# Fused four-block image kernel: the pieces of a normalised unit each one place later, four unit slots, loads two ahead

## The reference, cut to what matters

```python
x = x + L0(_gn(x))        # windowed attention with a roll
x = x + relu((y - mean(y)) * rsqrt(var(y) + eps) * gamma + beta)   # y = grouped 3x3 conv of _gn(x); mean over ALL images
x = x + L2(_gn(x))        # 1x1 conv, 3x3 conv in four chained groups, 1x1 conv
x = x + L3(_gn(x))        # the same once more
```

## Time and profile before

| | |
|---|---|
| median of three runs | 2432.0 us |
| the profiled execution, device time | 2433.68 us |
| its span in the trace | 2431.9 us |
| TensorE busy | 2062.5 us (85%) |
| VectorE busy | 1672.6 us (69%) |
| ScalarE busy | 1166.5 us (48%) |
| GpSimd busy | 1068.4 us (44%) |
| mean granted TensorE clock | 0.941 |

### The profile page before, as it was taken

The page is one execution under the profiler, slowest core; times in us unless marked ns, Lnnn a source line. Parts: engine busy times, 40 slices in busy tenths (PEclk is TensorE's granted clock), DMA queues, the critical chain, the costliest instruction groups (busy, mean ns, idle before and its releaser), DMA issues. The chain is left out here.

```text
span 2431.9 us, 75176 instructions
## 1 busy us (share of the span) xinstructions
PE 2062.5 (85%) x30482; PEld 1083.4 (45%) x30482; DVE 1672.6 (69%) x3497; ACT 1166.5 (48%) x2603; POOL 1068.4 (44%) x1234
## 2 busy tenths in 40 slices
PE   5699989988998899859995377787999999999996
PEld 4455555555555555535553123232344443333332
DVE  5588999899899989962324665666667665655653
ACT  5577666666676676632222244333434443433430
POOL 0277777776777677749501442222112221111100
PEclk8799999999999999979997588898999999999997
DMA  8301111111111111112224655655444444444444
GB/s 229 105 26 46 48 34 48 37 47 33 49 35 48 34 48 36 48 43 72 94 95 172 233 184 145 212 172 173 124 140 131 136 133 106 130 118 120 121 100 104
DMA packets 259007, 243.82 MB, mean 100 GB/s; under 512 B 124784, under 2 KB 230512, under 8 KB 258672
## 3 DMA queue, kind: packets, MB, share of 16 engines
q1 hardware_dynamic: 258672, 239.09, 32.5%
HBM read 92.45 MB, written 89.65 MB: 75 GB/s over the span
## 5 line engine op out<-in xcount | busy, mean ns | idle before, releaser
L1226 POOL TENSOR_SCALAR l_x<-l_x,l_scale,l_shift 128x384 f32<-128x384 f32 x192 | 147.5, 770 | 573.8 <-PE banks L1644 573.8
L1602 PE MATMUL banks<-l_a,l_taps 128*32 128x384 f32 x3456 | 331.1, 517 | 60.2 <-ACT l_r L1298 60.2
L435 POOL TENSOR_TENSOR at_prob<-at_prob,at_inv 128x512 f32<-128x512 f32 x288 | 294.2, 1042 | 116.6 <-DVE at_inv L575 111.3
L501 ACT ACTIVATE at_prob<-at_prob 128x512 f32<-128x512 f32 x288 | 181.9, 632 | 307.4 <-DVE at_prob L565 307.4
L1617 PE MATMUL banks<-l_above,l_taps 128*32 128x384 f32 x1728 | 311.7, 494 | 11.3 <-ACT l_above L1313 9.8
L1309 ACT ACTIVATE l_above<-l_below 96x384 f32<-96x384 f32 x144 | 75.5, 524 | 510.5 <-issue 274.9
L1617 PE MATMUL banks<-l_below,l_taps 128*32 128x384 f32 x1728 | 310.7, 495 | 0.0
L617 PE MATMUL banks<-at_xn,at_w 128*64 128x256 f32 x2336 | 286.1, 387 | 1.8 <-ACT at_xn L453 1.4
L1602 PEld LDWEIGHTS banks<-l_a,l_taps 128*32 128x32 f32 x3456 | 122.2, 115 | 243.8 <-issue 243.8
L1474 DVE COPY l_old<-l_a 32x384 f32<-32x384 f32 x576 | 221.7, 385 | 11.5 <-DVE l_bias L1431 0.2
L656 PE MATMUL banks<-const,at_prob 128*128 128x128 f32 x1152 | 183.8, 287 | 51.2 <-POOL at_prob L435 50.1
(11 more groups left out here) (160 smaller groups left out, 3598.0 us busy)
## 6 DMA issues: line engine op xcount, KB each, us to landing
l_x<-both SPq DMA_DIRECT2D x48, 768.0 KB, 4.4
l_rows<-l_r SPq DMA_DIRECT2D x768, 48.0 KB, 2.0
l_work<-both SPq DMA_DIRECT2D x36, 768.0 KB, 5.5
at_k_bd<-at_k SPq DMA_DIRECT2D x584, 32.0 KB, 1.8
load_raw<-in_x SPq DMA_DIRECT2D x36, 512.0 KB, 5.0
both<-c_y SPq DMA_DIRECT2D x96, 192.0 KB
both<-l_x SPq DMA_DIRECT2D x24, 768.0 KB, 3.9
out<-l_x SPq DMA_DIRECT2D x24, 768.0 KB, 4.5
```

The lines of the kernel that those rows point to most:

```text
L435: nc.gpsimd.tensor_tensor(prob[i][p][:, :, :], prob[i][p][:, :, :], inv[i][p][:, :].unsqueeze(2).broadcast_to([P, HEADS, WIN]), ALU.mult). ...
L501: nc.scalar.activation(prob[j % 2][p][:, :, :], prob[j % 2][p][:, :, :], ACT.Exp).then_inc(s["exped"], 1)
L1602: last = nc.tensor.matmul(grid(acc(k)[block_rows(c), :]), e[kind_of(k)][:, dy + 1, dx, :], a[:, k % A_RING, rows_, dx:dx + SIDE], start=(d ...
```

## The change

The unit's pieces are set apart. VectorE counts the unit of place (k, 0) at the end of step k, behind the last `update`, and those of places (k, 1) and (k, 2) in step k+1, behind its first `update`. GpSimd adds each unit one place later (place p's unit at p+1), behind one more `scale_x`. There are four slots in place of three, and at place n unit n+2 is loaded, after unit n-2 was counted and its store landed. The wait that frees a slot of image 0's units for the first loads is written for any number of slots.

```diff
-WORK_UNITS = 3
+WORK_UNITS = 4
@@ work_load, the first use of a slot
-                        used(FIRST_UNITS - 2 * WORK_UNITS + 2 * i)
-                        used(FIRST_UNITS - 2 * WORK_UNITS + 2 * i + 1)
+                        for slot in (2 * i, 2 * i + 1):
+                            used((FIRST_UNITS - 1 - slot) // (2 * WORK_UNITS) * 2 * WORK_UNITS + slot)
@@ work_move
-                    if n + 1 >= WORK_UNITS:
-                        work_load(n + 1)
+                    if n + 2 >= WORK_UNITS:
+                        work_load(n + 2)
@@ GpSimd's loop
                     scale_x(STRIP_T * k + p + TILE_LEAD)
-                    work_add(k, p)
+                    work_add(k, p - 1)
@@ VectorE's loop
                 update(at)
                 keep_out(at - 1)
+                work_count(k - 1, 1)
+                work_count(k - 1, 2)
...
                 update(at + 1)
                 keep_out(at)
-                work_count(k, 0)
                 find_delta(k - 3, 2)
...
                 update(at + 2)
                 keep_out(at + 1)
-                work_count(k, 1)
                 keep_old(k, 2, (0, 1))
                 find_delta(k, 0)
...
                 update(at + 3)
                 keep_out(at + 2)
-                work_count(k, 2)
+                work_count(k, 0)
```

## The result

| | before | after | ratio, 95% interval |
|---|---|---|---|
| median of four runs | 2430.97 us | 2355.73 us (2355.52 to 2356.15) | 0.9694 (0.9681 to 0.9706) |
| the profiled execution | 2433.68 us | 2355.57 us | |

A forecast was written before the change was run, and what follows sets the result against it. Units' work on VectorE, GpSimd and ScalarE was taken to delay keep_r, idling TensorE and slowing its clock; at the start, units bound. Sum: 2433.7 - 49 - 2 - 23 - 12 = 2348 us, range 2325 to 2386.

The forecast's parts named there:

- The bound and the mechanism: Steps 6 to 13: dense waits 47.2 us for ScalarE's late keep_r; with counts moved, some 10.
- A plain step, 18.8 us: Step with units, no norm: 17.4 us plus 1.4 from count and copy standstill; bounds 17.4 and 20.6.
- the walk: Walk through a step from step 16's times: of 2.5 us count and standstill, 1.4 reach dense.
- `find_delta` beside an add costs 0: End of a step: an add on find_delta(k, 0) does not stop it; 0 taken, other side 1.82 us.
- both adds on the path: Rival: both adds delay dense, 20.6 us a step, 22 us more, 2370 us; chance 0.17.
- The rule named in the prediction: VectorE and GpSimd share a port pair: two-port copies stand beside adds, single-SBUF-input instructions do not.
- Norm steps among units: Step 8's norm: 2.7 us more, once; steps 6 to 13 in all -49 us (-60 to -35).
- Step 14: Step with the last norm: 21.9 us falls to 20.1 without the slow clock, -2 us.
- Steps 2 to 5: Steps with less TensorE work: 89.8 us falls to 67, -23 us (-27 to -15).
- The start: Ahead of step 2: four slots let units pass sooner, step 2 begins near 1400, -12 us (-5 to -18).
- The DMA queue at 0: Unit load and turn issued later in a step: cost 0, with 1 to 2 us of cover.
- The adds' move: GpSimd's adds one place later: (k, 0) meets keep_old(k, 1), (k, 1) falls on find_delta(k, 0) and copies behind.

The follow-up runs named there:

- x1: The changed kernel with three slots, loads one ahead and adds as before, so only VectorE's counts have moved: 2355.87 us, ratio 0.9701.
- x2: The kernel before with four slots and the load of unit n+2, counts and adds unmoved: 2421.03 us, ratio 0.9961.
- x3: The kernel before with only GpSimd's adds one place later: 2425.50 us, ratio 0.9990.
- x5: The changed kernel with each GpSimd add cut to 8 of its 768 columns: 2337.05 us, ratio 0.9628.
- x4: The changed kernel with GpSimd's adds back at their old places: 2349.49 us, ratio 0.9667.
- x6: The changed kernel with the counts of (k-1, 1) and (k-1, 2) at the top of step k: 2345.61 us, ratio 0.9652.
- x12: x10 with the adds at their old place in steps that begin a norm, one place later in the others: 2327.82 us, ratio 0.9580.
- x7: The changed kernel with the norm of step 12 moved to step 16, where no units pass: 2351.75 us, ratio 0.9690.
- x8: The changed kernel with the edits of both x6 and x7: 2342.30 us, ratio 0.9649.
- x9: x8 with turn(k-5, 3) ahead of work_move(k, 0) in the DMA queue: 2336.90 us, ratio 0.9627.
- x10: x9 with the seven memsets of above, below and zero moved from VectorE to GpSimd: 2329.66 us, ratio 0.9591.

## Why the prediction came out as it did

- **The bound and the mechanism: right.** The count behind its add, ahead of `find_delta(k, 0)`, held `keep_r`. x1 moves only the counts and the wait, 41.9 us over eight steps in before, is 5.7; x2 and x3 leave the counts and keep 41.9 and 41.4. (The prediction set 47.2 us against steps 6 to 13; that figure has a ninth wait, the one ahead of step 14. The sum does not use it.)
- **A plain step, 18.8 us: right, 18.7 to 18.9.** Its 1.4 us over 17.4 came with the full adds, whose traces show the copies standing still as forecast, and x5 takes it away. The count, for which the walk allowed a part, had next to none in it. How the walk came to 1.4 of the possible 2.5 it does not say.
- **`find_delta` beside an add costs 0: right, 0.62 us in nine of nine,** and in every other such meeting in the kernels x1, x4 and x6 to x12. The rival "both adds on the path" is out. The rule named in the prediction (the Trainium skill, SBUF — State Buffer, section "Who interferes with whom") holds in both halves in this case's traces: copies from SBUF to SBUF stand until the add has ended (two of them take 2.16, 2.37 or 2.35 us), `find_delta`, with one SBUF tensor among its inputs, does not.
- **Norm steps among units: the term that failed.** The sum said 2.7 us over a plain step, read from step 18, and said it once. Two errors: step 12 also begins a norm while units still pass (the norm of image 0 for the next block) and the sum left it out; and a norm step costs 6.2 and 5.5 us over a plain one, not 2.7. Step 18 has no units, so its row could not show that a count would stand ahead of `norm_a`, or where the add of (k, 1) would fall. Plain steps give 5 x 18.8 = 94.0 and were 94.3; steps 8 and 12 were to be 21.5 + 18.8 = 40.3 and were 49.3; step 13 was 20.9 for 18.8. Together 11.4 us, and 164.5 - 153.1 is 11.4. x6 shows the part of the count (its wait back at 1.53), x7 what the second norm cost by its place (-2.5 at step 18), x12 the part of the add (-2.6 in steps 8 and 9). The bounds of the term, -60 to -35, held it.
- **Step 14: wrong by 3 us, by the same cause.** The count of the last unit of step 13 stands ahead of its `norm_a`, TensorE waits 2.58 us and the clock falls; in x6 and in x8 to x12 step 14 takes 20.2 to 20.3, the forecast's 20.1.
- **Steps 2 to 5: right in size,** 66.4 us for 67, and x1 (66.0) gives it to the counts. By its terms the forecast has 18.7 us for step 2 and 16.2 for step 4; they were 17.7 and 17.5, so some of the fit is luck.
- **The start: right in size (-12.3 for -12), in part by luck.** The slots, to which all of it was put down, give 8.7 alone; 3.6 came with the counts and the adds.
- **The DMA queue at 0: right for this kernel:** no f product waits for rows in steps 6 to 13, though rows landed in up to 6.3 us where the sum took 4.9 as the longest. x6 and x8 show what the later issue costs in shorter steps, x9 that the order in the queue was the cause.
- **The adds' move** was given no term of its own, only its effect on a step. x4 shows that it loses 4 to 6 us; a walk through steps 8 and 12 with the norm's pieces in their places might have met it.

## What to carry to other kernels

Price every kind of step apart, and list which steps carry the rare pieces before multiplying: here a uniform 8 x 18.8 was right for five steps and missed three. A rare piece measured in a step without the other load does not keep its price when both meet; walk that step's order on each engine. And when two engines share SBUF, shifting an add by one place matters less by its position than by which instruction of the other engine lies beneath it, so it is to be placed again after each other change. Last, an equal time is not an equal course: x1 and after have the same median, and differ by 10 us in each of two stretches.

## What was not expected of the hardware

- **The clock does not follow the length of the last wait alone.** In after, a wait of 2.58 us at 1509.75 was followed by the half clock, one of 2.74 at 1524.85 was not, and one of 2.20 at 1605.89 was, by the row below. Waits of 1.53 us at the same `norm_mean` never were (x6, x9, step 18). What sets these apart these rows do not settle.

```profile
1605.89 3.83 PE L1602 MATMUL banks<-l_a,l_taps 128*32 128x384 f32 x24 [2.20 <-ACT l_r L1298]
```

- **The one that comes second waits, copy or add.** Taken one by one, each of the 24 `keep_old` copies of after that start while an add runs ends 0.21 to 0.22 us after that add, however late in the add it started. A copy that is already under way when the add begins keeps its own time, in most cases 0.35 us, and then it is the add that is longer, up to 2.02 us in place of 1.83. So in x10 the first copy at 1507.15 was over at 1507.50, and only the second, which started 0.05 us into the add, stood until 1509.50.
- **48 KB transfers feel what was issued before them, with the channels 80% busy on average:** rows landed in up to 6.9 us behind a unit's store and load (x8), and in up to 5.0 ahead of them (x9); the quickest took 1.9 in both.
